# One burst of value products a step instead of two, with earlier normalisation and another bank for the last turned tile

## The reference

```
def _L0_cond_ref(x, emb, src_mask, norm_w, norm_b, q_w, q_b, k_w, k_b, v_w, v_b, ...):
    xn = layer_norm(x, norm_w, norm_b)
    q = (xn @ q_w + q_b).reshape(Bx, Tx, H, -1)
    k = (xn @ k_w + k_b).reshape(Bx, Tx, H, -1)
    att = jnp.einsum('bnhl,bmhl->bnmh', q, k)
    mask = src_mask.reshape(Bx, 1, Tx, 1)
    att = att + (1.0 - mask) * -1000000.0
    att = jax.nn.softmax(att, axis=2)
    v = ((xn @ v_w + v_b) * src_mask[:, :, None]).reshape(Bx, Tx, H, -1)
    y = jnp.einsum('bnmh,bmhl->bnhl', att, v).reshape(Bx, Tx, Dx)
    ...
```

## Time and profile before

| | |
|---|---|
| three timed runs | 2651.62, 2653.22, 2655.99 us |
| the profiled execution | 2654.44 us, its span 2652.6 us |
| TensorE busy | 2591.9 us (98%) |
| VectorE busy | 1817.8 us (69%) |
| ScalarE busy | 1251.5 us (47%) |
| GpSimd busy | 1345.1 us (51%) |

### The profile page before, as it was taken

The page is one execution under the profiler, slowest core; times in us unless marked ns, Lnnn a source line. Parts: engine busy times, 40 slices in busy tenths (PEclk is TensorE's granted clock), DMA queues, the critical chain, the costliest instruction groups (busy, mean ns, idle before and its releaser), DMA issues. The chain is left out here.

```text
span 2652.6 us, 43842 instructions
## 1 busy us (share of the span) xinstructions
PE 2591.9 (98%) x13634; PEld 1912.1 (72%) x13634; DVE 1817.8 (69%) x3277; ACT 1251.5 (47%) x2097; POOL 1345.1 (51%) x634
## 2 busy tenths in 40 slices
PE   7999999999999999999999789999999999999999
PEld 5666666666666666666663578888888888888887
DVE  6666666666666666666655777777777777777775
ACT  3555556555655566556655323333333333333333
POOL 1666666666666666666664234444343333443343
PEclk9999999999999999999999899999999999999999
DMA  6667666766676667666765411111111111111110
GB/s 146 97 86 108 100 101 85 106 100 101 85 106 101 101 85 106 101 101 85 106 101 152 152 33 53 52 52 52 52 52 49 47 40 43 35 50 52 49 35 32
DMA packets 141027, 211.44 MB, mean 80 GB/s; under 512 B 13944, under 2 KB 48812, under 8 KB 140988
## 3 DMA queue, kind: packets, MB, share of 16 engines
q1 hardware_dynamic: 104124, 143.82, 26.0%
q10 hardware_dynamic: 36864, 67.13, 19.1%
HBM read 74.87 MB, written 34.18 MB: 41 GB/s over the span
## 5 line engine op out<-in xcount | busy, mean ns | idle before, releaser
L809 ACT ACTIVATE probs<-exp_bank 128x512 f32<-128x512 f32 x1024 | 590.0, 598 | 504.2 <-PE exp_bank L553 431.5
L953 DVE TENSOR_REDUCE negmax<-max_bank 128x1 f32<-128x512 f32 x1024 | 680.7, 688 | 207.3 <-PE max_bank L538 205.9
L299 POOL TENSOR_TENSOR probs_sum<-probs_sum,probs 128x2048 f32<-128x2048 f32 x124 | 571.8, 4612 | 29.6 <-ACT probs L809 22.8
L299 POOL TENSOR_TENSOR probs_sum<-probs 128x2048 f32<-128x2048 f32 x63 | 289.4, 4594 | 496.4 <-ACT probs L809 496.4
L553 PE MATMUL exp_bank<-q_stack,k_stack 100*128 100x512 f32 x1024 | 422.3, 421 | 11.3 <-ACT probs L809 11.3
L538 PE MATMUL max_bank<-k_stack,q_stack 98*128 98x512 f32 x1024 | 417.5, 409 | 4.8 <-DVE negmax L953 2.3
L553 PEld LDWEIGHTS exp_bank<-q_stack,k_stack 100*128 100x128 f32 x1024 | 193.0, 189 | 137.8 <-ACT probs L809 52.7
L538 PEld LDWEIGHTS max_bank<-k_stack,q_stack 98*128 98x128 f32 x1024 | 192.8, 189 | 107.2 <-issue 54.5
L1650 POOL TENSOR_TENSOR sT_lo<-silu,sT_hi 128x512 fp32r<-128x512 f32 x124 | 164.9, 1345 | 188.1 <-DVE sT_hi L1798 188.1
L564 PE MATMUL y_bank<-probs,v_sb 128*32 128x512 f32 x2048 | 250.4, 607 | 0.0
L1645 POOL TENSOR_TENSOR rstd_y<-var_eps_y,b_minus_half 128x4 f32<-128x4 f32 x32 | 32.4, 1013 | 363.9 <-DVE var_eps_y L1734 363.9
(11 more groups left out here) (212 smaller groups left out, 5401.2 us busy)
## 6 DMA issues: line engine op xcount, KB each, us to landing
q_stack<-q_stage ACTq DMA_DIRECT2D x128, 256.0 KB
k_stack<-k_stage ACTq DMA_DIRECT2D x128, 256.0 KB
x_sb<-in_x SPq DMA_DIRECT2D x16, 1024.0 KB, 5.7
q_stack<-q_stage SPq DMA_DIRECT2D x64, 256.0 KB
k_stack<-k_stage SPq DMA_DIRECT2D x64, 256.0 KB
yT_scratch<-y_stage SPq DMA_DIRECT2D x64, 256.0 KB, 6.5
area<-yT_scratch SPq DMA_DIRECT2D x64, 256.0 KB, 4.4
area<-in_x SPq DMA_DIRECT2D x64, 256.0 KB, 2.8
```

The costliest lines, as they stand in the source:

```text
L299: eng.tensor_tensor(probs_sum[:, :, :], so_far, probs[:, mt, :, :], ALU.add).then_inc(probs_added, 1)
L809: act.activation(probs[:, mt, j, :], exp_bank[k % 2][:, :], ACT.Exp).then_inc(exp_done, 1)
L953: dve.tensor_reduce(negmax[:, m:m + 1], max_bank[m % 2][:, :], AXX, ALU.max, negate=True).then_inc(max_done, 1)
```

## The change

All value products and the sums stand behind exp 8, in slot 11: tiles 2 and 3 of the step before, its sums, then tiles 0 and 1 of the present step. ScalarE copies y in that slot too. ScalarE normalises x in slots 2 to 5 of group 1. The last two tiles of x are both turned in slot 10, and the last one goes to max_bank[0], behind the reduction of max 14, instead of a work bank; the low parts of these two are both in slot 11. GpSimd makes the inverse deviation between its first and second addition. ScalarE issues the two DMAs of q's high part in slots 4 and 5, one each, and those of k's in slot 8, each time behind that slot's exponential.

```diff
@@ -242,8 +242,15 @@
 
         QUARTERS = {"q": (0, 1, 2, 3), "k": (4, 5, 6, 7), "v": (9, 13, 14, 15)}
         VALUE_SLOTS_BESIDE_X = (14, 15, 15, 15)
-        X_TURNS = (8, 9, 10, 11)
-        X_LOWS = (8, 10, 11, 12)
+        X_TURNS = (8, 9, 10, 10)
+        X_LOWS = (8, 10, 11, 11)
+
+        def turned_in(k):
+            return [tt for tt in range(TT) if X_TURNS[tt] == k]
+
+        def bank_of_x(tt, static):
+
+            return max_bank[0] if static >= len(FIRST_USES) and tt == TT - 1 else work_bank[static % 2]
         MAX_TURN = 12
 
         FILM_TURNS = {(NG - 2, 13): (0, 0), (NG - 2, 14): (0, 1), (NG - 2, 15): (1, 0), (NG - 1, 0): (1, 1)}
@@ -277,6 +284,8 @@
         STACK_DMAS = 2 * 3 + 1
         HIGH_ROWS = {"q": (0, 2), "k": (0, 1)}
         LOW_ROW = {"q": 1, "k": 2}
+
+        HIGH_ISSUES = {"q": {4: slice(0, 1), 5: slice(1, 2)}, "k": {8: slice(0, 2)}}
 
         def stack_rows(n, row, g):
             dst = {"q": q_stack, "k": k_stack}[n]
@@ -466,9 +475,9 @@
                 add_probs(pool, s, 1, first)
                 if last and g == NG - 2:
                     return
-                add_probs(pool, s, 2)
                 if g == 0 and not last:
                     inverse_deviation(b + 1)
+                add_probs(pool, s, 2)
                 add_probs(pool, s, 3)
 
             inverse_deviation(0)
@@ -522,8 +531,12 @@
                 if stop:
                     last.then_inc(work_full, 1)
 
-            def transpose_x(tt, number):
-                out = take_bank(number)
+            def transpose_x(tt, number, beside_maxima=None):
+                if beside_maxima is None:
+                    out = take_bank(number)
+                else:
+                    pe.wait_ge(max_done, beside_maxima)
+                    out = max_bank[0][:, :]
                 for kt in range(KT):
                     last = pe.transpose(out[:, kt * P:(kt + 1) * P], x_sb[:, tt, kt * P:(kt + 1) * P], ident[:, :])
                 last.then_inc(work_full, 1)
@@ -684,7 +697,7 @@
 
                 exp_scores(b, g, e, first)
                 before = (b, g - 1) if g else (b - 1, NG - 1)
-                if e == 6 and not first:
+                if e == 8 and not first:
                     weigh_values(*before, 2)
                     weigh_values(*before, 3)
                     sum_probs(*before)
@@ -731,10 +744,11 @@
                             if kt == 0:
                                 banks[name] = take_bank(use(b, g, u, last))
                             project_quarter(what, tile, banks[name], kt, kt == 0, kt == KT - 1)
-                    if g == 1 and not last and k in X_TURNS:
-                        tt = X_TURNS.index(k)
-                        pe.wait_ge(xhat_done, TT * (b + 1) + tt + 1)
-                        transpose_x(tt, use(b, 1, f"x{tt}"))
+                    if g == 1 and not last:
+                        for tt in turned_in(k):
+                            pe.wait_ge(xhat_done, TT * (b + 1) + tt + 1)
+                            transpose_x(tt, use(b, 1, f"x{tt}"),
+                                        SLOTS * (step_of(b, 1) + 2) - 1 if tt == TT - 1 else None)
                     if has_next:
                         for m in maxima(k)[1:]:
                             max_scores(n_b, n_g, m)
@@ -769,7 +783,7 @@
             def high_of_x(tt, number, count):
                 act.wait_ge(work_full, number + 1)
                 act.activation(xT_hi[:, :, tt * P:(tt + 1) * P],
-                               work_bank[count % 2][:, :].rearrange("p (k t) -> p k t", k=KT),
+                               bank_of_x(tt, count)[:, :].rearrange("p (k t) -> p k t", k=KT),
                                ACT.Copy).then_inc(hi_done, 1)
 
             def high_of(what, g, number, count):
@@ -777,10 +791,10 @@
                 act.activation(stage[what][:, 0, :], work_bank[count % 2][:, :], ACT.Identity,
                                bias=bias[what][:, g:g + 1]).then_inc(hi_done, 1)
 
-            def stack_high(what, g, highs):
+            def stack_high(what, g, highs, part=slice(0, 2)):
 
                 act.wait_ge(hi_done, highs)
-                for row in HIGH_ROWS[what]:
+                for row in HIGH_ROWS[what][part]:
                     act.dma_start(stack_rows(what, row, g), stage[what][:, 0, :].bitcast(F32)).then_inc(stack_in[g], DMA)
 
             def mask_next_value(b, mt):
@@ -861,19 +875,20 @@
                     if not (first and g == 0 and k < LAG):
                         exp_slot(*exp_of(b, g, k), first and g == 0)
                     for what in "qk":
+                        if k in HIGH_ISSUES[what] and (not last or g < NG - 2):
+                            stack_high(what, (g + 2) % NG, high_count(b, g, "qk".index(what)), HIGH_ISSUES[what][k])
                         if k == QUARTERS[what][-1] and (not last or g < NG - 2):
 
                             p_b, p_g = (b, g + 1) if g + 1 < NG else (b + 1, 0)
                             act.wait_ge(stack_in[p_g], DMA * STACK_DMAS * (p_b + 1))
                             static, number = use(b, g, what, last)
                             high_of(what, (g + 2) % NG, number, static)
-                            stack_high(what, (g + 2) % NG, high_count(b, g, "qk".index(what)))
-                    if g == 1 and not last and k in X_TURNS:
-                        tt = X_TURNS.index(k)
-                        static, number = use(b, 1, f"x{tt}")
-                        high_of_x(tt, number, static)
-                    if g == 1 and not last and 5 <= k < 5 + TT:
-                        normalise_x(b + 1, k - 5)
+                    if g == 1 and not last:
+                        for tt in turned_in(k):
+                            static, number = use(b, 1, f"x{tt}")
+                            high_of_x(tt, number, static)
+                    if g == 1 and not last and 2 <= k < 2 + TT:
+                        normalise_x(b + 1, k - 2)
                     if k == 12 and g == 0 and not first:
                         mask_next_value(b, 2)
                     if k in (12, 14) and g == NG - 1 and not last:
@@ -925,7 +940,7 @@
             def low_of_x(tt, static, hi_count):
                 dve.wait_ge(hi_done, hi_count)
                 cols = slice(tt * P, (tt + 1) * P)
-                dve.tensor_tensor(xT_lo[:, :, cols], work_bank[static % 2][:, :].rearrange("p (k t) -> p k t", k=KT),
+                dve.tensor_tensor(xT_lo[:, :, cols], bank_of_x(tt, static)[:, :].rearrange("p (k t) -> p k t", k=KT),
                                   xT_hi[:, :, cols].bitcast(F32), ALU.subtract).then_inc(work_read, 1)
 
             def low_of(what, g, static, hi_count):
@@ -1069,9 +1084,9 @@
                     for i, what in enumerate("qk"):
                         if k == QUARTERS[what][-1] + 1 and (not last or g < NG - 2):
                             low_of(what, (g + 2) % NG, use(b, g, what, last)[0], high_count(b, g, i))
-                    if g == 1 and not last and k in X_LOWS:
-                        tt = X_LOWS.index(k)
-                        low_of_x(tt, use(b, 1, f"x{tt}")[0], high_count(b, 1, 2 + tt))
+                    for tt in range(TT):
+                        if g == 1 and not last and k == X_LOWS[tt]:
+                            low_of_x(tt, use(b, 1, f"x{tt}")[0], high_count(b, 1, 2 + tt))
                     if g == 0 and not last and k == 11:
                         statistics_of_tile(b + 1, 2)
                         statistics_of_tile(b + 1, 3)
```

## The result

The changed kernel takes **2736.73 us** (median of 4 runs, 2732.58 to 2741.3), the kernel before 2653.48 in the runs beside it: a ratio of 1.0313, 95% interval 1.0298 to 1.0328, or 83 us more. The forecast was 2720 us with a range of 2688 to 2775. The profiled execution took 2739.91 us, the one before 2654.44, so the two traces are 85.5 us apart.

The account below looks back on a forecast made before the run. TensorE was taken as the bound, busy 1281.5 of 1290.5 us. Group 0 adds 21.3, groups 2 and 3 with the last group 0 27.9, group 1 15.0: +64 on 2654.4 gives 2718, rounded to 2720 us; range 2688 to 2775.

Parts of the forecast that it names:

- The bank: Slot 9: without the first burst the value product waits for VectorE to read k's projection from its bank, 1.26 us.
- exp 6 to exp 8: TensorE's stretch between score matmuls for exponentials 6 and 8: forecast 3.23 us in groups 2 and 3, 3.85 in group 0.
- The first step of the kernel before: Has no burst in slot 9; its value product came 1.73 us after exp 6, taken as the model for the change.
- The copy of y: Inside the burst, tile 0 waits for ScalarE's copy; the sums' 0.85 us hide it, priced at 0, bounds 0 and 0.6.
- exp 8 to exp 9: TensorE's stretch holding the merged burst: 0.33 + 4.41 = 4.74 us; in group 1 0.41 ahead of the 4.41.
- Group 1: Steps that transpose the next batch's x: a late maximum delays exp 8, net 1.0 us more a step, bounds 0.4 and 2.5.
- exp 9 to exp 11: TensorE's later stretch in group 1: without x3's high part going ahead on ScalarE, 0.24 us comes back from 1.42.
- The issues: ScalarE's later DMA issues shorten the wait around exp 3: 0.10 us a step back, bounds 0 and 0.20.
- The rival that they do not overlap with an exponential: ScalarE's DMA issues run behind the exponential: group 1 costs 2.5 us instead of 1.0, 2743 us; chance 0.12.
- The clock: Rival: waits drop TensorE's granted clock to 0.50; 25 steps cost 40 us more, 2760 us, all 62 give 2819; chance 0.17.
- The last three steps: Steps at the end with few or no projections, for which the forecast counted nothing.
- The faster rival: The burst is simply cheaper and the value bank free within 0.4 us of exp 6: 39 us less, 2615 us; chance 0.06.

Follow-up runs that it names:

- Filler: The changed kernel with exp 6's product made four more times in slot 9 of groups 0, 2 and 3: 2738.18 us.
- late statistics: The changed kernel with the statistics of tiles 0 and 1 of the next x moved from slot 9 to slot 11: 2730.47 us.
- late value product: The late statistics kernel with the first quarter of the value projection moved from slot 9 to slot 12 in groups 0, 2 and 3: 2735.6 us.
- late low part: The late value product kernel with VectorE's low part of k moved to slot 11 in groups 0, 2 and 3: 2714.03 us.
- the merge alone: The kernel before with only all value products, the sums and the copy of y put into slot 11: 2795.13 us, ratio 1.0525.

## Why the prediction was right, and where its sizes were off

**The bank.** The step on which the forecast rests held to the hundredth: exp 6 to exp 8 3.23 us forecast in groups 2 and 3, 3.23 and 3.24 measured; 3.85 forecast in group 0, 3.85 measured. The first step of the kernel before was a true specimen. Filler, late statistics, late value product and late low part show its parts one by one: idle time that TensorE does not set, statistics worth 0.6 us in group 0, then the bank, then the reductions behind it.

**The copy of y.** This term was mis-sized: priced at 0, it is 0.23 us in group 3. It is most of the difference in exp 8 to exp 9 (4.74 forecast; 5.01, 4.92 and 5.00 measured in groups 0, 2 and 3; in group 1 0.41 + 4.41 = 4.82 forecast, 5.15 measured): the medians of the hole are 0.24, 0.30, 0.14 and 0.22 us in groups 0 to 3. The differences times 15 each are 15 x (0.27 + 0.18 + 0.26 + 0.33) = 15.6 us of the 21 us between the forecast's +64 and the measured +85.5. The forecast said that the cover holds if the copy starts within 0.25 us of the sums. It starts 0.34 us after them: the last product of tile 3, the row says, ends at 424.95 (423.03 + 1.92), 0.18 us after the sums have started, and the copy follows 0.16 us later. In the kernel before, TensorE's row of the sums and ScalarE's row ahead of the copy are these:

```profile
401.55 1.04 PE L576 MATMUL sums_bank<-probs_sum,head_sel 128*32 128x512 f32 x8
401.02 1.09 ACT L809 ACTIVATE probs<-exp_bank 128x512 f32<-128x512 f32 x2 [1.35 <-issue]
```

The 0.18 us could be read there: the products of tile 3 end at 399.81 + 1.92 = 401.73. The copy starts at 401.99, 0.44 us after the sums, but it follows two exponentials without a pause, so that row does not show what the hand-over costs. I had the rows and subtracted neither.

**Group 1.** Forecast +1.0, measured +1.33, and nearly all of the 0.33 is the same hole: exp 6 to exp 8 took 4.28 us (4.3 forecast), exp 9 to exp 11 gave back 0.23 (0.24 forecast). The forecast had one wait there, at max 15, and not the 0.66 us of x1's transposes; these lie inside the 3.16 us from exp 6 to max 15 (3.18 forecast) and cost nothing of their own.

**The issues.** 0.10 us a step forecast, 0.09 measured. The rival that they do not overlap with an exponential is refuted by the rows at 419.55 and 419.69; group 1, to which it belonged, has them at 372.11 and 372.25. That the next activation waits for their end was in the forecast of group 1 (the high part of x0 behind 355.9) and came so (373.57 behind 373.46). That they hold up exp 8 in the other groups was not in my text; it became visible only when VectorE was out of the way.

**The clock.** A rival with 25 steps and 40 us came as two steps of group 0 and 3.2 us in the profiled run. The windows view of one of them, ahead of the burst and in it:

```profile
255.00:258.30 3.30, 2.18 (x7) 1.30 (x8) 3.30 (x6) 1.36 (x3) 0.00 (x0) 1.00 1.04 122
258.41:261.82 3.41, 3.41 (x18) 0.78 (x20) 2.07 (x4) 0.60 (x1) 0.00 (x0) 0.50 1.08 126
```

TensorE is busy for 2.18 of 3.30 us, then the clock is 0.50 for 3.41 us. Twelve steps of the same group and order kept 1.00, and no run here tells what picks the two. The Trainium skill ("TensorE: Matmul & The Clock Gate", A second HAM failure mode: psum-queue depth-cycling) describes a clock that goes to and fro when there are short idle times between groups of matmuls; this kernel agrees in 2 of 14 steps, the merge alone in group 1 of every batch. My text said that the 59 steps of the earlier trace rows have no such waits; in fact they have 15 of 0.60 us, one in each group 1, at 1.00.

**What was not in the sum.** The last three steps add 1.9 us, which I had put at nothing.

**The faster rival.** Its 39 us needed a free bank within 0.4 us of exp 6. Even with the statistics, the value product, the low part, one maximum and the issues all moved, exp 6 to exp 8 is 1.41 us, and that kernel without its new wait would be near 2682 us. The hole ahead of tile 0 was left in all of these, and no run took it away, so whether one burst can win without it stays open.

## What to carry to other kernels

Before merging two stretches of work, ask what the first one covers: here 0.37 us at the edges of a burst were traded for the time in which another engine caught up, and what it cost (1.26 us of wait, 0.11 us behind it, 0.23 us of hole) was four times the gain. Then ask what each covered wait would be with the cover gone, and go on to the next: VectorE's bank, its reductions, ScalarE's issues and the arrival of a stack stood one behind the other, each hidden by the one before. A cover of known length has to be compared with when the covered work can start, and that is read from the end of the last product, not from the start of the next.

## What the hardware showed that I had not expected

- Here a DMA issue on ScalarE runs beside an activation that was already begun (an issue of 1.21 us for two at 419.69, the exponential from 419.55 to 420.14), but the next activation starts only behind it (421.01): 0.87 us idle.
- The hand-over of a bank costs time in both directions: ScalarE's copy starts 0.16 us after the last product that it reads (424.95 to 425.11; medians of 0.07 to 0.22 in the four groups, and a product's end is modelled), TensorE's next product into that bank 0.14 us after the copy (425.71 to 425.85, the same in all groups).
- In the merge alone max 15 of group 1 waits 1.32 us instead of 0.66, and the granted clock is 0.50 behind it in each of the 15 batches, which costs 1.5 us in 16 instructions (3.39 for 1.92).
